# Selective scan with experts on 8 cores: one ring of seven buffers for dBu, h and h*C, delta in a ring of six quarters, 3 of 16 products h*C on GpSimd, silu in halves, u*D put into PSUM by ScalarE

## The chip, the cores and the metric

The kernel runs on all 8 cores of one Trainium2 chip, without exchange between them: core 2b+j does half j of sequence b. The time is that of the slowest core, in microseconds of the device; lower is better. Before the change it is 4211.43 us (median of 3 runs, 4205.42 to 4250.64).

## What is computed

One layer of a state-space block (16 states per channel, 2048 inner channels, model width 1024) and a mixture of experts (16 routed, 2 taken per token; 2 shared), on 4 sequences of 4096 tokens:

```python
x_and_res = x @ W_in                                # 1024 -> 2 x 2048
xi, res = jnp.split(x_and_res, 2, axis=-1)
xc = conv(xi, conv_w, 4 taps, causal, per channel) + conv_b
xi = silu(xc)                                       # called u below
Bm, Cm = jnp.split(xi @ W_xproj, 2, axis=-1)        # 16 + 16 columns
delta = softplus(xi @ W_dt + b_dt)
A = -exp(A_log)
def step(h, inp):
    dA = exp(d_i[:, None, :] * A[None, :, None])
    h = h * dA + d_i[:, None, :] * B_i[:, :, None] * u_i[:, None, :]
    y_i = sum(h * C_i[:, :, None], axis=1)
y = ys + xi * D_param
y = y * silu(res)
x = layernorm(x + y @ W_out)
# then: scores, softmax, top 2, x + routed + shared experts, layernorm
```

A core owns 2048 tokens. It walks 4096: a first half of 2048 that only builds up the state h (zeros, with a flag of 0, for the cores that own the start of a sequence), and a second half for which y is made.

## The kernel before, in words

Time is cut into 16 chunks k of 256 tokens (`TA`); chunks 0 to 7 (`PK`) are the first half, chunks 8 to 15 the second, "real" one. The 2048 channels are 16 tiles of 128; four tiles make a quarter of 128 x 1024 values (`QW`). A chunk has 64 steps: four quarters q of 16 states n. A step `st` handles one state of one quarter. `NR0` = 512 is the first real step.

What one step issues, engine by engine:

- GpSimd (`pool_front`, L522) multiplies du (= delta*u) of the quarter by the broadcast row B of state n into one of `NB` = 3 buffers `dBu`. It waits that the scan has freed the buffer. After n = 8 it prepares the next quarter (`prepare`: du by L442, and zt = delta*A of the first token, L445). After n = 13 it makes the next quarter's 16 carried-in states (`carry_in`, L459 to L467), for which it waits on an Exp by ScalarE (`first_decay`, L800). After the dBu of step 27 of a chunk it casts u of the next chunk to bf16 (`cast_u`, L433).
- ScalarE (`act_front`) does, in this order in each step: `keep_carry(st)` (L829, the last token's h is kept; in the second half it waits for the product), `decay(st+2)` (L817, exp(delta*A) into PSUM, three steps ahead in the first half), `give_carry(st+2)` (L838, the carried state into column 0 of dBu), then `dense(k, s)`: the evacuation of whatever group of matmuls stands in this step. After n = 11 comes `first_decay` of the next quarter. At step 26 it does the silu of the four quarters of u of chunk k+1, at steps 12 and 26 those of res.
- VectorE (`dve_front`) runs the scan (L942: h = decay*h + dBu) over 4 x 256 columns; in the second half it writes h over the decay in PSUM and then makes the product h*C in one of `NY` = 2 buffers `ym` (L952). At the first step of the next quarter it makes `combine`: u*D added in PSUM (L918, four instructions) and times silu(res) (L930).
- TensorE (`pe_front`) runs at each step first the group that `stage_at` names, then, in the second half, the accumulation of the product into the PSUM area `YB` by a product with the identity (L728, two of 512 columns). Its queue is in order, so the group of step s+1 stands behind the accumulation of step s.

The groups are those of the next chunk (k+1): input projection `xi` (L680, steps 0, 3, ..., 21), convolution `cv` (L692, steps 2, 5, ..., 23), `bc` = B and C (L701, step 30), `dt` = delta (L710, 16 groups at steps 32 to 59, about every 1.8th); and, in real chunks, `rs` = res of the same chunk (L680, steps 1, 4, ..., 22). Each goes to one of two PSUM banks and is evacuated by ScalarE in the same step of its own order. Chunk 0 has all of them 14 steps later, and part of its own `dt` groups in its steps (`LATE`). Weights are streamed by SyncE from bf16 copies in memory into rings of three (`x`) and two (`cv`, `dt`).

Semaphores alone bind the engines; the order on each is written out by hand in these functions. The lines that matter most:

```python
for key in stage_at(k, s):
    run(key)                                   # TensorE: the group of this step
if k >= 0 and is_real(k):
    te.wait_ge(s_ym, r + 1)                    # then the product of this step
```

```python
keep_carry(st)                                 # ScalarE, one step
decay(st + 2)
give_carry(st + 2)
dense(k, s)                                    # waits for the group of this step
if n == (12 if k == 0 else 11) and q + 1 < NQ:
    first_decay(q + 1)
```

## Time and profile before

| | |
|---|---|
| median of the runs | 4211.43 us |
| the profiled execution | 4194.85 us, span 4193.3 us (its slowest core, core 7; cores 4142.5 to 4193.3) |
| busy, share of the span | TensorE 2616.4 us (62%), VectorE 3296.4 (79%), ScalarE 2085.7 (50%), GpSimd 2779.4 (66%) |
| mean granted clock of TensorE | 0.846 on core 7, 0.845 on both dies |
| chain that ended last | VectorE 38%, issue 27%, GpSimd 11%, TensorE 10%, DMA 9%, ScalarE 2% |

The span has four stretches: a start of 124 us, the first half of the scan (512 steps, to about 1524 us), the second half (512 steps, to about 3556 us), and output projection, router and experts (637 us), which the change leaves alone but for how many token tiles are fetched early (`NPRE`). In the slices of the page VectorE is at eight to nine tenths in both halves; GpSimd is at nine tenths in the first half and six in the second. A busy share tells how much an engine worked, not which wait ended last.

### The profile page before, as it was taken

To read this page: it belongs to the slowest core of one execution; us is meant where nothing else is said; L and a number is where in the kernel's file an instruction comes from. 1 tells how busy PE (TensorE), PEld (TensorE's weight loads), DVE (VectorE), ACT (ScalarE), POOL (GpSimd) and SP (SyncE) were. 2 spreads that over 40 slices of the span, in tenths; PEclk is the share of its full clock that TensorE was granted. 3 is DMA by queue.
4 is the path that set the end of the run, shared out by engine and by line. 5 is a ranking of instruction groups with operands and counts; after the bars stand their busy time and mean duration, and the time that the engine had idled before them with its cause. 6 is when DMAs were issued, how large, how long until landed. Compare 5 with 4: busy or idle time off the path is not lost.

```text
span 4193.3 us, 57121 instructions; the slowest of 8 cores (4142.5 to 4193.3 us)
## 1 busy us (share of the span) xinstructions
PE 2616.4 (62%) x12773; PEld 1473.4 (35%) x12773; DVE 3296.4 (79%) x2266; ACT 2085.7 (50%) x4748; POOL 2779.4 (66%) x1556
## 2 busy tenths in 40 slices
PE   3354544444434467776777877777787665867870
PEld 2243332333323343343433434344443321433430
DVE  1678888888888898978989999898998999542227
ACT  2566666666666665445554645545455443210210
POOL 1889999999999986656666676666666665011012
PEclk8777776777767689989999999999999999888985
DMA  7653546635444356663736546464441321214976
GB/s 158 172 173 117 159 118 169 162 114 160 124 140 129 89 141 116 148 140 77 171 99 149 146 98 164 107 151 116 123 119 54 81 61 70 101 61 169 304 280 201
DMA packets 197735, 569.57 MB, mean 136 GB/s; under 512 B 21624, under 2 KB 87928, under 8 KB 175248
## 3 DMA queue, kind: packets, MB, share of 16 engines
q1 hardware_dynamic: 164736, 433.44, 33.7%
q0 software_dynamic: 32656, 132.36, 15.0%
q8 instruction: 117, 1.92, 0.2%
q14 instruction: 226, 1.85, 0.2%
HBM read 529.25 MB, written 154.14 MB: 163 GB/s over the span
## 4 chain that ended last, share of the span: by engine, by line
DVE 38%; issue 27%; POOL 11%; PE 10%; DMA 9%; ACT 2%; DVEq 1%; another core or an unknown queue 1%; POOLq 0%; SPq 0%; ACTq 0%
DVE PP L942 23%; DVE ym L942 8%; POOL dBu L522 8%; PE PP L1180 3%; DVE ym L952 2%; DMA RA<-wbx 2%; PE PP L1074 2%; DMA RA<-wbd 1%; PE PP L728 1%; DVE PP L918 1%; PE PP L1131 1%; DMA r<-xs 1%; DMA RA<-W_inx 1%; PE PP L710 1%
## 5 line engine op out<-in xcount | busy, mean ns | idle before, releaser
L522 POOL TENSOR_TENSOR dBu<-du,bcl 128x1020 f32<-128x1020 f32 x1024 | 2377.3, 2346 | 449.9 <-DVE PP L942 449.3
L942 DVE TENSOR_TENSOR_SCAN ym<-PP,dBu 128x1024 f32<-128x1024 f32 x512 | 1168.0, 2289 | 288.3 <-POOL dBu L522 263.3
L728 PE MATMUL PP<-ym,sid 128*128 128x512 f32 x2048 | 1048.8, 638 | 485.9 <-DVE ym L952 485.7
L942 DVE TENSOR_TENSOR_SCAN PP<-PP,dBu 128x1024 f32<-128x1024 f32 x512 | 1171.5, 2288 | 64.6 <-POOL dBu L522 52.4
L817 ACT ACTIVATE PP<-d,negA 128x1020 f32<-128x1020 f32 x1024 | 1124.8, 1099 | 2.3 <-issue 1.2
L710 PE MATMUL PP<-xib,RA 128*128 128x256 bf16 x4096 | 580.9, 305 | 310.6 <-ACT d L771 218.3
L952 DVE TENSOR_TENSOR ym<-PP,bcl 128x1024 f32<-128x1024 f32 x512 | 626.7, 1224 | 114.7 <-DVE PP L942 79.5
L728 PEld LDWEIGHTS PP<-ym,sid 128*128 128x128 f32 x2048 | 364.7, 198 | 966.6 <-issue 963.5
L710 PEld LDWEIGHTS PP<-xib,RA 128*128 128x128 bf16 x4096 | 438.1, 109 | 501.3 <-issue 414.4
L680 PE MATMUL PP<-xb,RA 128*128 128x256 bf16 x3072 | 450.7, 310 | 111.8 <-ACT d L771 35.8
L829 ACT ACTIVATE carry<-PP 128x4 f32<-128x4 f32 x512 | 88.4, 173 | 857.5 <-DVE ym L952 857.3
L680 PEld LDWEIGHTS PP<-xb,RA 128*128 128x128 bf16 x3072 | 339.6, 111 | 265.9 <-issue 190.2
L692 PE MATMUL PP<-xiraw,RA 128*128 128x256 bf16 x1024 | 168.6, 319 | 296.3 <-ACT xiraw L748 292.2
L829 ACT ACTIVATE carry<-ym 128x4 f32<-128x4 f32 x448 | 93.0, 208 | 422.0 <-DVE ym L942 420.8
L692 PEld LDWEIGHTS PP<-xiraw,RA 128*128 128x128 bf16 x1024 | 108.5, 111 | 378.2 <-issue 354.9
L838 ACT ACTIVATE dBu<-hc 128x4 f32<-128x4 f32 x1024 | 197.1, 193 | 0.0
L1242 ACT ACTIVATE r<-PP 128x1024 bf16<-128x1024 bf16 x48 | 49.0, 1024 | 278.6 <-PE PP L1166 278.6
L1180 PE MATMUL PP<-RA,r 128*128 128x512 bf16 x768 | 178.7, 387 | 9.2 <-DVE r L1446 8.1
L1446 DVE COPY r<-PP 128x1024 f32<-128x1024 f32 x48 | 58.7, 1225 | 158.4 <-DMA ys<-r 86.4
L984 POOL DMA_INDIRECT RA<-wre,widx x16 | 15.2, 948 | 228.9 <-PE PP L1180 228.1
L977 POOL DMA_INDIRECT xs<-r,posi x32 | 31.1, 973 | 189.6 <-DVE widx L1434 181.2
L442 POOL TENSOR_TENSOR du<-d,RA 128x1024 f32<-128x1024 f32 x64 | 150.5, 2351 | 1.6 <-ACT d L795 1.6
(149 smaller groups left out, 1821.5 us busy)
## 6 DMA issues: line engine op xcount, KB each, us to landing
RA<-wbd SPq DMA_DIRECT2D x120, 1024.0 KB, 6.5
RA<-wbx SPq DMA_DIRECT2D x184, 512.0 KB, 4.2
bcl<-bc_hbm SPq DMA_DIRECT2D x128, 256.0 KB, 6.8
wre<-Wre POOLq DMA_DIRECT2D x16, 2048.0 KB, 18.1
RA<-wbc SPq DMA_DIRECT2D x120, 256.0 KB, 3.0
ys<-r SPq DMA_DIRECT2D x48, 512.0 KB
xs<-g SPq DMA_DIRECT2D x26, 768.0 KB, 6.8
bcl<-bc_hbm SPq DMA_DIRECT2D x128, 128.0 KB, 5.2
```

What stands on the lines that cost most here:

```text
L442: ge.tensor_tensor(du[q % 2][:], quarter(d_b[k % 2], qd), quarter(u_b[k % 2], qd), ALU.mult).then_inc(s_du, 1)
L522: ge.tensor_tensor(ct3(dBu[st % NB][:])[:, :, 1:TA], ct3(du[q % 2][:])[:, :, 1:TA], bcl[n][:, 1:TA].rearrange("p (o t) -> p o t", o=1) .br ...
L680: mm = te.matmul(b[:, c * TA:(c + 1) * TA], wx[j % NX][:, (c * 8 + q) * 128:(c * 8 + q + 1) * 128], xb[k % 2][:, q * TA:(q + 1) * TA], sta ...
L692: mm = te.matmul(b[:, c * TA:(c + 1) * TA], wcv[j % NCV][:, (c * 4 + tap) * 128:(c * 4 + tap + 1) * 128], xr3[:, 2 * p + c, tap:tap + TA], ...
L710: mm = te.matmul(b[:, 0:TA], wdt[j % NDT][:, (c * CT + q) * 128:(c * CT + q + 1) * 128], xib[:, q * TA:(q + 1) * TA], start=(q == 0), stop ...
L728: mm = te.matmul(YB[:, zb * 512:(zb + 1) * 512], sid128[:], ym[r % NY][:, zb * 512:(zb + 1) * 512], start=(n == 0), stop=(n == NST - 1))
L817: se.activation(out=ct3(dec[b])[:, :, 1:TA], in_=ct3(quarter(d_b[k % 2], q % 4))[:, :, 1:TA], func=AF.Exp, scale=negA[:, n:n + 1]).then_in ...
L829: se.activation(out=carry[:, s * QC:(s + 1) * QC].rearrange("p (c o) -> p c o", o=1), in_=ct3(src)[:, :, TA - 1:TA], func=AF.Copy, scale=( ...
L838: se.activation(out=ct3(dBu[st % NB][:])[:, :, 0:1], in_=hc[q % 2][:, n * QC:(n + 1) * QC].rearrange("p (c o) -> p c o", o=1), func=AF.Cop ...
L942: ve.tensor_tensor_scan(out=hout, data0=dec[b], data1=dBu[st % NB][:], initial=0.0, op0=ALU.mult, op1=ALU.add).then_inc(s_scan, 1)
L952: ve.tensor_tensor(ct3(ym[r % NY][:]), ct3(dec[b]), bcl[n][:, TA:2 * TA].rearrange("p (o t) -> p o t", o=1) .broadcast_to([128, QC, TA]), ...
L1180: mm = te.matmul(pb[2 * (i % 2) + h], xT_r[i % 3][:, k * 128:(k + 1) * 128], wslot_e[b % 3][:, k * D + h * 512:k * D + (h + 1) * 512], sta ...
```

## The change

- One ring `hb` of `NB` = 7 buffers takes the place of `dBu` (3) and `ym` (2). dBu is made in a buffer, the scan reads it, the product h*C is made in the same buffer, TensorE accumulates from it. A buffer is free when TensorE has accumulated it (first half: when its last column is kept).
- The products of n = 1, 6 and 11 of each quarter (`POOL_N`) are made by GpSimd, which does so `LAG` = 4 steps later in its order: after the dBu of n = 5, 10 and 15. For these the scan writes h into the ring's buffer and not into PSUM. TensorE waits for each product in the order of the steps, whoever makes it.
- u*D: ScalarE writes it into `YB` at the first step of a quarter (`seed_y`, four instructions, after `give_carry`, ahead of `dense`), once the quarter before is combined. TensorE's accumulations of a quarter all add to it (a product once at the start sets the banks' state); the first waits for it. `combine` keeps only the multiplication by silu(res).
- delta is kept in a ring of six quarters (`dring`) in place of two whole chunks.
- For chunks 8 to 15: the silu of u is made in two halves, at steps 13 and 26; the cast to bf16 by GpSimd in two halves, ahead of the dBu of steps 22 and 36; `bc` at step 38, `dt` at steps 39, 40, 41, 43, 44, 46, 47, 49, 50, 51, 53, 54, 56, 57, 59, 60. The silu of the first half of res moves from step 12 to 13.
- For chunks 0 to 7 ScalarE makes the cast, after the four silus at step 26.
- At the start GpSimd issues two fetches of `dt` weights at its steps 0 and 1, no longer ahead of its first `prepare`; `NPRE` is 8, was 10.

```diff
@@ -35,13 +35,15 @@
...
-NPRE = 10
+NPRE = 8
...
-NB = 3
-NY = 2
+NB = 7
+LAG = 4
+ND = 6
+POOL_N = (1, 6, 11)
@@ -70,8 +72,15 @@
...
+def bc_step(k):
+
+    return 38 if k + 1 >= PK else 30 + shift(k)
+
+
 def dt_step(k, c):
+    if k + 1 >= PK:
+        return 39 + (23 * c) // 16
     return 46 + c if k == 0 else 32 + (29 * c) // 16
@@ -86,7 +95,7 @@
...
-        if f == 30:
+        if s == bc_step(k):
@@ -136,6 +145,21 @@
...
+
+
+def on_pool(r):
+
+    return r % NST in POOL_N
+
+
+def n_pool(r):
+
+    return r // NST * len(POOL_N) + sum(r % NST >= n for n in POOL_N)
+
+
+def n_dve(r):
+
+    return r + 1 - n_pool(r)
@@ -202,7 +226,7 @@
...
-    d_b = [sf(f"d{i}", [128, CT * TA], F32) for i in range(2)]
+    dring = sf("dring", [128, ND * QW], F32)
...
@@ -285,6 +307,7 @@
...
+    d_of = lambda q: dring[:, (q + 2) % ND * QW:((q + 2) % ND + 1) * QW]
...
@@ -401,6 +427,28 @@
...
+    def u_cast(e, k):
+
+        if is_real(k):
+            e.wait_ge(s_xibr, 4 * (k - PK + 1))
+        else:
+            e.wait_ge(s_xib, 4 * (k + 1))
+
+    def product_done(e, r):
+
+        if on_pool(r):
+            e.wait_ge(s_yp, n_pool(r))
+        else:
+            e.wait_ge(s_ym, n_dve(r))
+
+    def buffer_free(e, st):
+
+        p = st - NB
+        if p >= NR0:
+            e.wait_ge(s_ya, p - NR0 + 1)
+        elif p >= 0:
+            e.wait_ge(s_car, p + 1)
+
     def load_g(sy, j):
@@ -425,12 +473,19 @@
...
-        def cast_u(k):
-            if k >= 1:
-                ge.wait_ge(s_mm, USE[("dt", k - 1, CT - 1)] + 1)
-            for qd in range(4):
+        def cast_u(k, half):
+            ge.wait_ge(s_mm, USE[("dt", k - 1, CT - 1)] + 1)
+            for qd in (2 * half, 2 * half + 1):
                 ge.wait_ge(s_u, 4 * k + qd + 1)
-                ge.tensor_copy(quarter(xib, qd), quarter(u_b[k % 2], qd)).then_inc(s_xib, 1)
+                ge.tensor_copy(quarter(xib, qd), quarter(u_b[k % 2], qd)).then_inc(s_xibr, 1)
+
+        def product(st):
+            r, n = st - NR0, st % NST
+            ge.wait_ge(s_scan, st + 1)
+            ge.wait_ge(s_car, st + 1)
+            ge.tensor_tensor(ct3(hb[st % NB][:]), ct3(hb[st % NB][:]),
+                             bcl[n][:, TA:2 * TA].rearrange("p (o t) -> p o t", o=1)
+                             .broadcast_to([128, QC, TA]), ALU.mult).then_inc(s_yp, 1)
...
@@ -491,10 +546,7 @@
...
-        cast_u(0)
...
-        for p in range(2, 4):
-            cast_weights(("dt", 0, 2 * p))
@@ -502,26 +554,26 @@
...
             q, n = st // NST, st % NST
-            if k == 0 and s in (12, 28):
-                for p in range(2):
-                    cast_weights(("dt", 0, (8 if s == 12 else 12) + 2 * p))
+            if k == 0 and s in (0, 1, 12, 13, 28, 29):
+                cast_weights(("dt", 0, {0: 4, 1: 6, 12: 8, 13: 10, 28: 12, 29: 14}[s]))
             if k == 2 and s == 2:
...
                 ge.dma_start(out=wbx[8 + s // 8], in_=W_inx[8 + s // 8]).then_inc(s_wres, 16)
-            if s == 28 + shift(k) and k + 1 < NK:
-                cast_u(k + 1)
+            if PK <= k + 1 < NK and s in (22, 36):
+                cast_u(k + 1, s // 36)
             if s == 40 and k + 2 < NK:
...
             ge.wait_ge(s_du, q + 1)
-            if st >= NB:
-                ge.wait_ge(s_scan, st - NB + 1)
-            ge.tensor_tensor(ct3(dBu[st % NB][:])[:, :, 1:TA], ct3(du[q % 2][:])[:, :, 1:TA],
+            buffer_free(ge, st)
+            ge.tensor_tensor(ct3(hb[st % NB][:])[:, :, 1:TA], ct3(du[q % 2][:])[:, :, 1:TA],
                              bcl[n][:, 1:TA].rearrange("p (o t) -> p o t", o=1)
                              .broadcast_to([128, QC, TA - 1]), ALU.mult).then_inc(s_dbu, 1)
+            if st - LAG >= NR0 and on_pool(st - LAG - NR0):
+                product(st - LAG)
             if n == 5:
@@ -529,6 +581,9 @@
...
                     carry_in(q + 1)
+        for st in range(NS - LAG, NS):
+            if on_pool(st - NR0):
+                product(st)
@@ -558,7 +613,7 @@
...
-                    sy.wait_ge(s_ym, last - NR0 + 1)
+                    product_done(sy, last - NR0)
...
@@ -652,9 +708,9 @@
...
-                if s == 32 + shift(k):
+                if s == bc_step(k) + 2:
...
-                if s == 34 + shift(k):
+                if s == bc_step(k) + 4:
...
@@ -714,6 +770,11 @@
...
+        for zb in range(2):
+            for i in range(4):
+                mm = te.matmul(YB[:, zb * 512 + i * 128:zb * 512 + (i + 1) * 128], sid128[:], sid128[:],
+                               start=(i == 0), stop=(i == 3))
+        mm.then_inc(s_bits, 1)
@@ -721,13 +782,13 @@
...
                     n = s % NST
-                    te.wait_ge(s_ym, r + 1)
-                    if n == 0 and r >= NST:
-                        te.wait_ge(s_g, r // NST)
+                    product_done(te, r)
+                    if n == 0:
+                        te.wait_ge(s_yd, r // NST + 1)
                     for zb in range(2):
                         mm = te.matmul(YB[:, zb * 512:(zb + 1) * 512], sid128[:],
-                                       ym[r % NY][:, zb * 512:(zb + 1) * 512],
-                                       start=(n == 0), stop=(n == NST - 1))
+                                       hb[(k * NSTEP + s) % NB][:, zb * 512:(zb + 1) * 512],
+                                       start=False, stop=(n == NST - 1), skip_group_check=True)
                     mm.then_inc(s_ya, 1)
@@ -750,9 +811,9 @@
...
-                    se.wait_ge(s_xib, 4 * (k - 1))
+                    u_cast(se, k - 2)
...
-                        se.wait_ge(s_cb, 16 * (k - 2 - PK + 1))
+                        se.wait_ge(s_yd, 4 * (k - 2 - PK + 1))
@@ -765,10 +826,12 @@
...
-                if k >= 2:
-                    se.wait_ge(s_z, 4 * (k - 1))
-                    se.wait_ge(s_dA, (k - 1) * NSTEP)
-                se.activation(out=d_b[k % 2][:, p * TA:(p + 1) * TA], in_=b[:, 0:TA],
+                q = 4 * k + p // 4
+                if q >= ND:
+                    se.wait_ge(s_du, q - ND + 1)
+                    se.wait_ge(s_z, q - ND + 1)
+                    se.wait_ge(s_dA, (q - ND + 1) * NST)
+                se.activation(out=d_of(q)[:, p % 4 * TA:(p % 4 + 1) * TA], in_=b[:, 0:TA],
@@ -776,12 +839,19 @@
...
-        def silu_u(k):
-            se.wait_ge(s_ev, USE[("cv", k, 7)] + 1)
-            for qd in range(4):
+        def silu_u(k, half):
+            se.wait_ge(s_ev, USE[("cv", k, 4 * half + 3)] + 1)
+            for qd in (2 * half, 2 * half + 1):
                 se.activation(out=quarter(u_b[k % 2], qd), in_=quarter(u_b[k % 2], qd),
                               func=AF.Silu).then_inc(s_u, 1)
-            if k + 1 < NK:
+            if not is_real(k):
+                if k >= 1:
+                    se.wait_ge(s_mm, USE[("dt", k - 1, CT - 1)] + 1)
+                for qd in (2 * half, 2 * half + 1):
+                    se.wait_ge(s_u, 4 * k + qd + 1)
+                    se.activation(out=quarter(xib, qd), in_=quarter(u_b[k % 2], qd),
+                                  func=AF.Copy).then_inc(s_xib, 1)
+            if half == 1 and k + 1 < NK:
                 se.wait_ge(s_mm, USE[("cv", k, 7)] + 1)
...
@@ -805,8 +875,11 @@
...
-                se.wait_ge(s_ym, st - NR0 - 1)
-                se.wait_ge(s_car, st - 1)
+                if on_pool(st - 2 - NR0):
+                    se.wait_ge(s_scan, st - 1)
+                else:
+                    se.wait_ge(s_ym, n_dve(st - 2 - NR0))
+                    se.wait_ge(s_car, st - 1)
@@ -815,29 +888,42 @@
...
             se.activation(out=ct3(dec[b])[:, :, 1:TA],
-                          in_=ct3(quarter(d_b[k % 2], q % 4))[:, :, 1:TA],
+                          in_=ct3(d_of(q))[:, :, 1:TA],
                           func=AF.Exp, scale=negA[:, n:n + 1]).then_inc(s_dA, 1)
...
             se.wait_ge(s_scan, st + 1)
-            if st >= NR0:
-                se.wait_ge(s_ym, st - NR0 + 1)
+            in_psum = st >= NR0 and not on_pool(st - NR0)
+            if in_psum:
+                se.wait_ge(s_ym, n_dve(st - NR0))
             if st >= NSTEP:
                 se.wait_ge(s_hc, st // NST + 1)
-            src = dec[decay_slot(st)] if st >= NR0 else h_b[st % 2][:]
+            src = dec[decay_slot(st)] if in_psum else hb[st % NB][:]
             se.activation(out=carry[:, s * QC:(s + 1) * QC].rearrange("p (c o) -> p c o", o=1),
...
             q, n = st // NST, st % NST
-            if st >= NB:
-                se.wait_ge(s_scan, st - NB + 1)
+            buffer_free(se, st)
             se.wait_ge(s_hc, q + 1)
-            se.activation(out=ct3(dBu[st % NB][:])[:, :, 0:1],
+            se.activation(out=ct3(hb[st % NB][:])[:, :, 0:1],
                           in_=hc[q % 2][:, n * QC:(n + 1) * QC].rearrange("p (c o) -> p c o", o=1),
                           func=AF.Copy).then_inc(s_pad, 1)
+
+        def seed_y(q):
+            k, qd, r = q // 4, q % 4, q - 4 * PK
+            if r == 0:
+                se.wait_ge(s_scan, max(t for t in range(NR0) if decay_slot(t) == 2) + 1)
+            else:
+                se.wait_ge(s_g, r)
+            for c in range(QC):
+                ct = qd * QC + c
+                ins = se.activation(out=YB[:, c * TA:(c + 1) * TA],
+                                    in_=u_b[k % 2][:, ct * TA:(ct + 1) * TA],
+                                    func=AF.Copy, scale=Dp_c[:, ct:ct + 1])
+            ins.then_inc(s_yd, 1)
@@ -851,15 +937,14 @@
...
             if k + 1 < NK:
-                if s == 26 + shift(k):
-                    silu_u(k + 1)
+                for half in range(2):
+                    if s == (13 if half == 0 and k + 1 >= PK else 26) + shift(k):
+                        silu_u(k + 1, half)
             if k >= 0 and is_real(k):
-                if s == 12:
-                    silu_res(k, 0)
-                    silu_res(k, 1)
-                if s == 26:
-                    silu_res(k, 2)
-                    silu_res(k, 3)
+                for half in range(2):
+                    if s == (13, 26)[half]:
+                        silu_res(k, 2 * half)
+                        silu_res(k, 2 * half + 1)
@@ -879,12 +964,15 @@
...
                 give_carry(st + 2)
+            if st >= NR0 and n == 0:
+                seed_y(q)
             dense(k, s)
...
         ve.memset(xr3[:, :, 0:3], 0.0).then_inc(s_halo, 1)
+        ve.wait_ge(s_bits, 1)
         for i in range(3):
@@ -911,17 +999,8 @@
...
         def combine(q):
-            k, qd, r = q // 4, q % 4, q - 4 * PK
+            qd, r = q % 4, q - 4 * PK
             ve.wait_ge(s_ya, NST * (r + 1))
-            for c in range(QC):
-                ct = qd * QC + c
-                ve.scalar_tensor_tensor(
-                    out=YB[:, c * TA:(c + 1) * TA],
-                    in0=u_b[k % 2][:, ct * TA:(ct + 1) * TA],
-                    scalar=Dp_c[:, ct:ct + 1],
-                    in1=YB[:, c * TA:(c + 1) * TA],
-                    op0=ALU.mult, op1=ALU.add).then_inc(s_cb, 1)
-            ve.wait_ge(s_cb, QC * (r + 1))
             ve.wait_ge(s_sr, r + 1)
@@ -936,20 +1015,15 @@
...
             ve.wait_ge(s_pad, st + 1)
-            if st >= 2 and r < 0:
-                ve.wait_ge(s_car, st - 1)
-            hout = dec[b] if r >= 0 else h_b[st % 2][:]
-            ve.tensor_tensor_scan(out=hout, data0=dec[b], data1=dBu[st % NB][:], initial=0.0,
+            by_dve = r >= 0 and not on_pool(r)
+            hout = dec[b] if by_dve else hb[st % NB][:]
+            ve.tensor_tensor_scan(out=hout, data0=dec[b], data1=hb[st % NB][:], initial=0.0,
                                   op0=ALU.mult, op1=ALU.add).then_inc(s_scan, 1)
...
                 combine(q - 1)
-            if r >= 0:
+            if by_dve:
                 ve.wait_ge(s_scan, st + 1)
-                if r < 2:
-                    ve.wait_ge(s_car, NR0 - 1 + r)
-                if r >= NY:
-                    ve.wait_ge(s_ya, r - NY + 1)
-                ve.tensor_tensor(ct3(ym[r % NY][:]), ct3(dec[b]),
+                ve.tensor_tensor(ct3(hb[st % NB][:]), ct3(dec[b]),
                                  bcl[n][:, TA:2 * TA].rearrange("p (o t) -> p o t", o=1)
...
```

## Rows read from the trace of the kernel before

**Rows 1.** Busy time by stretch: start, first half, second half, rest (us, instructions, clock, DMA)

```profile
124.00:1524.00 1400.00, 651.56 (x3888) 457.43 (x3888) 1166.58 (x512) 910.84 (x1995) 1335.70 (x727) 0.72 0.48 139
1524.00:3556.00 2032.00, 1507.66 (x6300) 789.90 (x6300) 1844.80 (x1180) 1047.97 (x2555) 1344.52 (x721) 0.94 0.46 116
```

**Rows 2.** Waits of the second half (total us, times, longest us)

```profile
POOL dBu L522 <- DVE PP L942: 449.3, 304, 7.6
...
POOL zt L459 <- ACT zt L800: 121.8, 22, 9.2
...
DVE PP L942 <- POOL dBu L522: 52.4, 9, 7.5
```

**Rows 3.** Timeline of VectorE over a quarter's change (start us, us, instruction)

```profile
2429.88 2.29 DVE L942 TENSOR_TENSOR_SCAN PP<-PP,dBu 128x1024 f32<-128x1024 f32 x1
...
2434.08 1.23 DVE L930 TENSOR_TENSOR g<-PP,sres 128x1024 bf16<-128x1024 f32 x1 [0.24 <-DVE PP L918]
...
2436.35 2.29 DVE L942 TENSOR_TENSOR_SCAN PP<-PP,dBu 128x1024 f32<-128x1024 f32 x1
...
2439.95 2.29 DVE L942 TENSOR_TENSOR_SCAN PP<-PP,dBu 128x1024 f32<-128x1024 f32 x1
```

**Rows 4.** Timeline of VectorE in the first half: six scans that wait for nothing

```profile
788.89 13.80 DVE L942 TENSOR_TENSOR_SCAN ym<-PP,dBu 128x1024 f32<-128x1024 f32 x6 [1.10 <-POOL dBu L522]
```

**Rows 5.** Timeline of GpSimd in a quarter of the second half, around carry_in

```profile
2455.50 2.35 POOL L442 TENSOR_TENSOR du<-d,RA 128x1024 f32<-128x1024 f32 x1
...
2471.20 2.35 POOL L522 TENSOR_TENSOR dBu<-du,bcl 128x1020 f32<-128x1020 f32 x1 [1.25 <-DVE PP L942]
...
2478.34 0.32 POOL L459 TENSOR_TENSOR zt<-zt,carry 128x64 f32<-128x64 f32 x1 [4.79 <-ACT zt L800]
...
2479.43 9.27 POOL L522 TENSOR_TENSOR dBu<-du,bcl 128x1020 f32<-128x1020 f32 x4
```

**Rows 6.** Timeline of ScalarE at n = 11 and 12 of that quarter

```profile
2476.20 0.17 ACT L829 ACTIVATE carry<-PP 128x4 f32<-128x4 f32 x1 [1.64 <-DVE ym L952]
...
2477.71 0.24 ACT L800 ACTIVATE zt<-zt 128x64 f32<-128x64 f32 x1
...
2481.32 0.45 ACT L771 ACTIVATE d<-PP,colt 128x256 f32<-128x256 f32 x1
```

**Rows 7.** Timeline of TensorE in the second half, back to back and after idle times

```profile
2381.91 1.04 PE L692 MATMUL PP<-xiraw,RA 128*128 128x256 bf16 x8
...
2469.00 1.96 PE L728 MATMUL PP<-ym,sid 128*128 128x512 f32 x4
2470.79 1.91 PE L710 MATMUL PP<-xib,RA 128*128 128x256 bf16 x16
...
2419.30 6.37 PE L728 MATMUL PP<-ym,sid 128*128 128x512 f32 x8 [8.92 <-DVE ym L952]
...
2532.08 3.57 PE L710 MATMUL PP<-xib,RA 128*128 128x256 bf16 x16 [4.23 <-DMA RA<-wbd]
```

**Rows 8.** Timeline of ScalarE at step 26 of a real chunk

```profile
2406.45 1.28 ACT L782 ACT_TABLE_LOAD   x1
...
2407.74 3.90 ACT L782 ACTIVATE RA<-RA 128x1024 f32<-128x1024 f32 x4
...
2414.00 1.28 ACT L817 ACT_TABLE_LOAD   x1
```

**Rows 9.** Timeline of GpSimd in a chunk of the first half, around the cast

```profile
734.10 3.98 POOL L433 CAST xib<-RA 128x1024 bf16<-128x1024 f32 x4 [3.82 <-ACT RA L782]
...
742.66 0.31 POOL L459 TENSOR_TENSOR zt<-zt,carry 128x64 f32<-128x64 f32 x1
```

**Rows 10.** Timeline of ScalarE there: the Exp that carry_in waits for

```profile
739.50 0.24 ACT L800 ACTIVATE zt<-zt 128x64 f32<-128x64 f32 x1
```

**Rows 11.** Timeline of GpSimd at the start

```profile
116.63 0.53 POOL L426 DMA_DIRECT2D RA<-W_dtx  x1 [22.16 <-DMA wbd<-RA]
...
121.70 27.63 POOL L522 TENSOR_TENSOR dBu<-du,bcl 128x1020 f32<-128x1020 f32 x12 [0.21 <-issue]
```

21 lines of the change are left out of this document (12 added, 9 removed).

## The prediction

> **What bounds the kernel now.** I read the stretches first, then the waits, then the timelines. The first half's 512 steps take 1400 us with GpSimd busy for 1335.7 of them; the second half's take 2032 us with VectorE busy for 1844.8 and GpSimd for 1344.5 [rows 1]. So each half has its own bound, and the change shifts work from the engine that bounds the second one. The waits of the second half agree: GpSimd waits 449.3 us for scans to free its three buffers, but also 121.8 us for the Exp ahead of carry_in; VectorE waits for dBu only nine times, 52.4 us in all [rows 2]. The timelines give pitches, which count more than durations since neighbours overlap. From scan to scan it is 3.60 us, with a quarter's change in between 6.47, so combine costs 2.87 [rows 3]. A scan that waits for nothing takes 13.80/6 = 2.30 us [rows 4]. A chunk's work on VectorE is thus 64 x 3.60 + 4 x 2.87 = 241.9 us, of 2032/8 = 254 measured; 12 us are stalls, the longest (7.5 us, [rows 2]) after the silus of step 26.
>
> **VectorE's work after.** Per quarter: 12 steps of 3.60; n = 0 with a scan (2.30), one multiplication by silu(res) (about 1.2, [rows 3]) and a product (1.2), 4.7 together; three bare scans, 6.9. Sum 54.8 us, 219 a chunk, 23 less than now. Over eight chunks 183 us would be gained if nothing made VectorE wait. What follows asks whether that holds.
>
> **The steps around n = 11.** Let T be the end of scan 11, whose product GpSimd now makes. In this order:
> - ScalarE keeps the carry, makes decay and pad of step 13, and the Exp of the next quarter; from the carry's start that took until 2477.95, 1.75 us [rows 6], and with the group's evacuation (0.45, [rows 6]) and the handover about 2.7. So the Exp ends at T+2.7, if TensorE isn't late.
> - GpSimd has had dBu 13 for long and waits (now 4.79 us there, [rows 5]). Its next dBu starts 2479.43 - 2477.95 = 1.5 us after the Exp. It then makes dBu 14 and 15 (9.27/4 = 2.32 each) and only then product 11, priced as the same kind of instruction, 2.35 [rows 5]. That ends 8.5 us after the Exp: T+11.2. However deep the ring is, carry_in takes GpSimd's lead away here in every quarter.
> - TensorE stands at product 11 all that time, in order. Behind it are the group of step 12 and the products of 12 to 15, which VectorE has ready. Each accumulation or group of 16 takes about 1.8 us back to back, a convolution's group of 8 about 1.1 [rows 7].
> - ScalarE stands in `dense(12)` for that group: accumulation 1.8, group 1.9, handover and evacuation 0.7, then carry, decay and pad of step 15, 1.6 (2477.71 - 2476.20 and a handover, [rows 6]). VectorE wants them at T+10.8 (three steps of 3.60) and gets them at T+17.4. A stall of 6.6 us. Where step n = 12 has a group, that is steps 12, 44 and 60, three quarters of four.
> - combine must have product 15 accumulated. Unstalled it would start at T + 4 x 3.60 + 2.30 = T+16.7; five accumulations and the groups between them end at T+20.2 or later.
>
> **A chunk quarter by quarter** (from combine to combine; without stalls T comes at 54.8 - 16.7 = 38.1 us). *Steps 48 to 63*: scan 15 at T+17.5, scan 16 ends at T+23.4, TensorE is done by then. T is 38.6, since `seed_y` delays the first accumulation and the carries of n = 1 to 4 a little: 62.1 us. *Steps 32 to 47*: groups at n = 6 to 9, 11, 12, 14, 15. With 3.6 us of TensorE in most of these steps it is late by T, the evacuation of step 11 too, so the Exp is at T+4.6, product 11 at T+13.0, and the accumulation of 15 at T+27.6: 37.9 + 27.7 = 65.6. *Steps 16 to 31*: none at n = 12, but at step 26 ScalarE still has two silus of u and two of res between two table loads. Now there are four and two (1.28, 3.90, ..., 1.28 in [rows 8]). Without two of them the Exp is at T+7.7, product 11 at T+16.1, five accumulations end at T+25.3: 64.5. *Steps 0 to 15*: a group in every step, the Exp at T+4.9, product 11 at T+13.3; the evacuation of step 13 comes after three more of TensorE's pieces and then four silus (5.2 us with a table load) and a load back, so decay 16 is ready only at T+29.5: 39.0 + 32.1 = 71.1. Sum 263.3 against 254 now. In chunk 15 there are only the groups of res and no silu of u; the same walk gives 64 + 61 + 58 + 58 = 241 against 253.
>
> Second half at full clock: 7 x 9.3 - 12 = +53.
>
> **The clock.** In the second half TensorE's clock is granted at 0.94 of full speed [rows 1]. After a wait of 8.92 us two accumulations took 6.37 us, where two back to back take 3.7; after one of 4.23 us a group took 3.57, where others take 1.91 [rows 7]: the lower level, 1.2 GHz. The change puts a wait of 6 to 9 us into each of 32 quarters, right before the chain that counts. The price is from 0 (clock kept, as in the accumulation of 1.96 us, [rows 7]) to 2.6 us each; I take 1.66, the nearer row's 3.57 - 1.91: +53. By the Trainium skill, "TensorE: Matmul & The Clock Gate", Part 1, the array falls to half clock when it idles and comes back after a while of work; the rows agree. Its remark that the ramp costs under 1% of a typical kernel's span would cap this term at 42 us, the sum at 4296.
>
> **The first half.** The cast leaves GpSimd (3.98 us and a wait of 3.82 before it, [rows 9]), which looks like 7.8 us a chunk. But GpSimd then arrives sooner at carry_in, which waits for the Exp; and ScalarE has four casts more (3.9 us, as its silus, [rows 8]) between silu and that Exp. It ends at 739.74 now [rows 10], then at 743.65, and carry_in starts at 744.1 and not 742.66 [rows 9]: +1.4 us a chunk, six times; +1.9 in chunk 0; about -0.5 in chunk 7, whose next chunk is cast the other way. The ring of seven helps no more than one of three where GpSimd is the bound. At the start GpSimd no longer stands at the fetch issued at 116.63 [rows 11] before `prepare`, but it stands there one dBu later, and the casts by ScalarE cost about 2.7 us: second dBu at 120 rather than 124, -4. Together +6.
>
> The seed's start matmuls lie in the wait for the first weights; four seed instructions and a smaller combine are in the walk; two token tiles fetched later (`NPRE`) have the output projection of the tiles before them as cover, 0. SyncE's fetch of bcl waits for GpSimd's product, with weight fetches queued behind it; those are due steps later, 0. `dt` groups 1.44 steps apart leave less room for their weights: 0 to +5 us a chunk, taken as 0. GpSimd's sixteen dBu, three products, prepare and carry_in are some 49 us of 54.8: not the bound by sum.
>
> **Sum**: 4194.85 + 53 + 53 + 6 = 4307 us. The profiled execution is 0.4% under the median of 4211.43 shown; I leave that in the range.
>
> **Rivals.** *(a) The other side: the ring covers it.* GpSimd keeps a lead over n = 11 to 15, so that product 11 comes within some 4 us of its scan, and the group of step 12 in time for scan 15 (that is the point: 6.6 us earlier than walked). Then only today's stalls stay: 4194.85 - 183 + 6 = 4018. For it: GpSimd's 449.3 us of waiting for buffers [rows 2] go, and 49 us fit into 54.8. Against it: the buffers don't free ScalarE from `dense(12)`. The Trainium skill, "Perfetto Trace Analysis", Optimizing Scalar/DVE Operations, says that moving work from a saturated VectorE even to GpSimd may make sense, and warns of the port that they share. *(b) Half of it.* ScalarE's two steps of slack and the removed combine cancel the lateness: stalls of 6 us a quarter and no clock loss give 243 a chunk, 4194.85 - 84 + 6 = 4117; with 8.6, as walked but without the clock, 4254. *(c) Slower than the forecast.* Late accumulations also meet the weights' fetches and the low clock twice a quarter (the wait of the first accumulation for `seed_y` is some 5 us too): +1.7 in 24 quarters and +5 in 7 chunks: 4383. It decides wherever TensorE's queue and not VectorE ends last. *(d)* The change does less than it says: product on GpSimd slower than dBu (in place, VectorE writing the same memory). At 3.5 us instead of 2.35 it adds 1.2 in 32 quarters: 4344.
>
> **Chances.** Forecast, with (d), 0.48; (c) 0.14; (a) 0.17; (b) 0.21, of which 0.14 near 4250 and below, within 1% of the median (4169 to 4253, about what a measurement here can tell from no change), and 0.07 faster. So faster 0.24, same 0.14, slower 0.62. The range leaves out the ideal case and the far end of (c): 4110 to 4385; the forecast's own is 4254 (no loss of clock) to 4350.
>
> **What would show it.** GpSimd's product for n = 11 starts right after a dBu, about 9 us after the scan; TensorE idle for 6 to 9 us before the accumulation of n = 11, then half clock; ScalarE's wait for TensorE in `dense` high, which is small now; a stall of VectorE ahead of scan 15 and 16; no gap there in chunk 15's last quarters. GpSimd's wait for VectorE small. A chunk at 263 to 275 us. Wrong if VectorE's gaps at n = 15 are under 2 us, a chunk is under 245 us, or the first half's chunks fall below 173.

## The result and the profile after

The changed kernel takes 4419.56 us (median of four runs, 4411.96 to 4421.41) beside 4208.43 for the one before on the same chip: 1.0493 times as long, 95% interval 1.0447 to 1.054. The forecast was 4307 with 4385 as its upper end; direction and mechanism came out, the size didn't: +211 us, not +96 (profiled execution against profiled execution, as the forecast was summed: 4421.41 - 4194.85 = +227 for +112). In some executions the cores of one die are granted a lower clock and take longer: ratios, the times of runs 2, 3 and 8 and the ranges over cores leave these out, the other medians have them in. This is the head of its page (busy time; then busy tenths in 40 slices):

```profile
span 4419.8 us, 56272 instructions; the slowest of 8 cores (4351.3 to 4419.8 us)
...
PE 2653.0 (60%) x12745; PEld 1523.3 (34%) x12789; DVE 3133.7 (71%) x2042; ACT 2157.6 (49%) x4910; POOL 2962.5 (67%) x1620
...
DVE  1878887878888857677686777767787788652227
...
PEclk7777676776776888888888888889888887888985
...
PE 29%; issue 21%; POOL 16%; DVE 15%; DMA 10%; ACT 7%; another core or an unknown queue 1%; POOLq 1%; DVEq 0%; ACTq 0%; SPq 0%
```

VectorE lost 163 us of work against before (3296.4) and the span still grew by 226.5: an engine that has less to do and takes longer is waiting. Its digits show where, after the middle (6 and 7 where before had 8 and 9), and PEclk has mostly an 8 there where before had a 9. The last line is the chain that ended last: TensorE leads it with 29%, where before it was VectorE with 38%. The stretches (start to first scan, first half, second half, rest) answer to [rows 1]:

```profile
0.00:106.00 106.00, 46.63 (x288) 33.69 (x288) 14.88 (x74) 30.27 (x49) 14.58 (x24) 0.81 0.75 167
106.00:1515.00 1409.00, 644.39 (x3920) 456.27 (x3920) 1167.57 (x512) 939.41 (x2026) 1309.12 (x699) 0.72 0.49 141
1515.00:3787.00 2272.00, 1554.58 (x6304) 839.96 (x6304) 1685.80 (x961) 1087.72 (x2683) 1556.85 (x817) 0.84 0.41 103
```

The second half took 2272 us against 2037 (1525 to 3562; [rows 1] leaves off its last 6): +235. It starts 10 us earlier than before. Waits of the second half (total, times, longest), which answer to [rows 2]:

```profile
DVE PP L1020 <- ACT hb L911: 447.1, 101, 27.4
PE PP L789 <- POOL hb L486: 393.0, 46, 16.4
ACT dring L834 <- PE PP L766: 384.7, 112, 12.7
POOL zt L514 <- ACT carry L903: 289.2, 22, 34.0
...
PE PP L789 <- ACT PP L923: 186.4, 32, 13.6
POOL hb L572 <- PE PP L789: 72.0, 56, 24.9
...
PE PP L736 <- DMA RA<-wbx: 57.0, 7, 26.5
```

Read as a ring: VectorE waits for ScalarE's `give_carry` (L911), which ScalarE issues right after the decay (447), ScalarE for TensorE's group (385), TensorE for GpSimd's product (393). GpSimd's old wait for VectorE's scans (449.3 in [rows 2]) is gone, as the ring of seven promises; nobody needed it. One quarter, steps 32 to 47 of a chunk, from combine to combine. GpSimd and TensorE:

```profile
2583.75 0.33 POOL L500 TENSOR_TENSOR zt<-dring,negA 128x64 f32<-128x64 f32 x1
2584.04 4.64 POOL L572 TENSOR_TENSOR hb<-du,bcl 128x1020 f32<-128x1020 f32 x2
2588.64 2.33 POOL L486 TENSOR_TENSOR hb<-hb,bcl 128x1024 f32<-128x1024 f32 x1
...
2609.89 0.32 POOL L514 TENSOR_TENSOR zt<-zt,carry 128x64 f32<-128x64 f32 x1 [12.02 <-ACT carry L903]
...
2610.98 4.63 POOL L572 TENSOR_TENSOR hb<-du,bcl 128x1020 f32<-128x1020 f32 x2
2615.57 2.35 POOL L486 TENSOR_TENSOR hb<-hb,bcl 128x1024 f32<-128x1024 f32 x1
```

```profile
2591.12 3.47 PE L789 MATMUL PP<-hb,sid 128*128 128x512 f32 x4 [3.73 <-POOL hb L486]
...
2618.06 3.75 PE L789 MATMUL PP<-hb,sid 128*128 128x512 f32 x4 [9.43 <-POOL hb L486]
2621.60 2.17 PE L766 MATMUL PP<-xib,RA 128*128 128x256 bf16 x16
```

ScalarE and VectorE in the same quarter (T, the end of scan 11, is 2602.67 + 2.28 = 2604.95):

```profile
2609.26 0.25 ACT L870 ACTIVATE zt<-zt 128x64 f32<-128x64 f32 x1
...
2624.04 0.47 ACT L834 ACTIVATE dring<-PP,colt 128x256 f32<-128x256 f32 x1 [11.93 <-PE PP L766]
```

```profile
2564.76 1.23 DVE L1009 TENSOR_TENSOR g<-PP,sres 128x1024 bf16<-128x1024 f32 x1 [5.75 <-PE PP L789]
...
2599.12 2.30 DVE L1020 TENSOR_TENSOR_SCAN PP<-PP,hb 128x1024 f32<-128x1024 f32 x1 [2.91 <-ACT hb L911]
...
2602.67 2.28 DVE L1020 TENSOR_TENSOR_SCAN hb<-PP,hb 128x1024 f32<-128x1024 f32 x1
...
2626.11 2.30 DVE L1020 TENSOR_TENSOR_SCAN PP<-PP,hb 128x1024 f32<-128x1024 f32 x1 [8.92 <-ACT hb L911]
...
2634.39 1.23 DVE L1009 TENSOR_TENSOR g<-PP,sres 128x1024 bf16<-128x1024 f32 x1 [2.45 <-PE PP L789]
```

The Exp ends at T+4.6 and the product of n = 11 (behind carry_in and two dBu) at 2617.92, T+13.0: to a tenth what the walk of this quarter had. Then comes the accumulation at 1.2 GHz (3.75 us, 1.88 at 2.4 GHz), the group ScalarE stands for, scan 15, and combine at T+29.4 (walked 27.7 + 1.66). What the walk did not have is the line at 2591.12: the product of n = 6 is late too, behind `prepare` and two dBu, and costs TensorE 3.73 us of waiting, the lower level once more, and VectorE the 2.91 us at 2599.12. T came at 40.2 us after combine, not 37.9.

Distances from combine to combine, read off VectorE's timeline, in us (L930 before, L1009 after; the starred quarters have a copy of the later stages' weights, issued by GpSimd at n = 5, that shows):

| chunk | before | after |
|---|---|---|
| k = 8 | –, 67.7, 65.0*, 60.5 | –, 95.1*, 67.8, 65.7 |
| k = 9 | 79.2*, 67.8, 60.5, 60.5 | 97.9*, 67.0, 69.6, 75.8* |
| k = 12 | 61.9, 68.1, 60.5, 60.5 | 74.1, 68.3, 70.8, 73.4* |
| k = 14, no copies | 61.9, 67.9, 60.5, 60.5 = 250.8 | 74.3, 66.8, 66.3, 65.7 = 273.1 |
| k = 15, no next chunk | 61.4, 61.9, 60.5, 60.5 = 244.3 | 67.3, 62.8, 58.4, 53.6 = 242.1 |

Chunk 15 has no dt groups, and there the saving of VectorE's work is all there in the last quarter: 53.6, with a pitch of 3.53 us from scan to scan (3.60 before).

### The profile page after: what moved, and what is told of

Its sections match the earlier page's. It is cut to its first block, busy times and chain, and to the rows that moved or that the text cites. A ratio compares the mean times of both kernels' runs of the same rounds, so it can differ in the third digit from the quotient of the medians.

```text
span 4419.8 us, 56272 instructions; the slowest of 8 cores (4351.3 to 4419.8 us)
## 1 busy us (share of the span) xinstructions
PE 2653.0 (60%) x12745; PEld 1523.3 (34%) x12789; DVE 3133.7 (71%) x2042; ACT 2157.6 (49%) x4910; POOL 2962.5 (67%) x1620
## 4 chain that ended last, share of the span: by engine, by line
PE 29%; issue 21%; POOL 16%; DVE 15%; DMA 10%; ACT 7%; another core or an unknown queue 1%; POOLq 1%; DVEq 0%; ACTq 0%; SPq 0%
PE PP L789 13%; POOL hb L572 11%; DVE hb L1020 7%; PE PP L766 5%; DVE PP L1020 4%; PE PP L736 4%; DMA RA<-wbx 3%; PE PP L1255 3%; POOL hb L486 2%; DMA r<-xs 2%; DMA RA<-wbd 2%; POOL du L497 2%; DVE hb L1026 1%; PE PP L1149 1%; PE PP L1206 1%
## 5 line engine op out<-in xcount | busy, mean ns | idle before, releaser
L572 POOL TENSOR_TENSOR hb<-du,bcl 128x1020 f32<-128x1020 f32 x1024 | 2370.8, 2347 | 73.3 <-PE PP L789 72.0
L1020 DVE TENSOR_TENSOR_SCAN hb<-PP,hb 128x1024 f32<-128x1024 f32 x608 | 1387.2, 2287 | 281.0 <-POOL hb L572 188.9
L789 PE MATMUL PP<-hb,sid 128*128 128x512 f32 x2048 | 1084.7, 668 | 623.5 <-POOL hb L486 393.0
L1020 DVE TENSOR_TENSOR_SCAN PP<-PP,hb 128x1024 f32<-128x1024 f32 x416 | 952.4, 2289 | 471.3 <-ACT hb L911 447.1
L890 ACT ACTIVATE PP<-dring,negA 128x1020 f32<-128x1020 f32 x1024 | 1124.9, 1099 | 1.2 <-issue 0.8
L789 PEld LDWEIGHTS PP<-hb,sid 128*128 128x128 f32 x2048 | 402.7, 213 | 1071.5 <-issue 1068.2
L1026 DVE TENSOR_TENSOR hb<-PP,bcl 128x1024 f32<-128x1024 f32 x416 | 509.3, 1224 | 40.1
L486 POOL TENSOR_TENSOR hb<-hb,bcl 128x1024 f32<-128x1024 f32 x96 | 225.4, 2348 | 251.0 <-ACT carry L903 250.9
L514 POOL TENSOR_TENSOR zt<-zt,carry 128x64 f32<-128x64 f32 x64 | 20.3, 318 | 446.4 <-ACT carry L903 353.3
L911 ACT ACTIVATE hb<-hc 128x4 f32<-128x4 f32 x1024 | 197.4, 193 | 0.0
L497 POOL TENSOR_TENSOR du<-dring,RA 128x1024 f32<-128x1024 f32 x64 | 151.1, 2361 | 48.7 <-ACT dring L865 48.7
```

Of the source, the lines that this page charges most:

```text
L486: ge.tensor_tensor(ct3(hb[st % NB][:]), ct3(hb[st % NB][:]), bcl[n][:, TA:2 * TA].rearrange("p (o t) -> p o t", o=1) .broadcast_to([128, Q ...
L497: ge.tensor_tensor(du[q % 2][:], d_of(q), quarter(u_b[k % 2], qd), ALU.mult).then_inc(s_du, 1)
L572: ge.tensor_tensor(ct3(hb[st % NB][:])[:, :, 1:TA], ct3(du[q % 2][:])[:, :, 1:TA], bcl[n][:, 1:TA].rearrange("p (o t) -> p o t", o=1) .bro ...
L789: mm = te.matmul(YB[:, zb * 512:(zb + 1) * 512], sid128[:], hb[(k * NSTEP + s) % NB][:, zb * 512:(zb + 1) * 512], start=False, stop=(n == ...
L890: se.activation(out=ct3(dec[b])[:, :, 1:TA], in_=ct3(d_of(q))[:, :, 1:TA], func=AF.Exp, scale=negA[:, n:n + 1]).then_inc(s_dA, 1)
L911: se.activation(out=ct3(hb[st % NB][:])[:, :, 0:1], in_=hc[q % 2][:, n * QC:(n + 1) * QC].rearrange("p (c o) -> p c o", o=1), func=AF.Copy ...
```

## The experiments

Each edit is against the changed kernel unless it says otherwise. "Before" is the kernel before on the same chip in the same hour.

**1. No products on GpSimd.**

```
-POOL_N = (1, 6, 11)
+POOL_N = ()
...
```

> The changed kernel with POOL_N empty: VectorE makes all 16 products h*C; ring, delta ring, schedule, seed by ScalarE as changed. Theory A (product 11 stands behind carry_in on GpSimd, which waits for ScalarE's Exp; TensorE stands at it, ScalarE in dense, VectorE for ScalarE): the boundary stalls of 6 to 16 us a quarter go, VectorE has 58.5 us of work a quarter, 32 x 58.5 = 1872 plus some 150 us of other stalls for the second half: about 4170 us. Theory B (what costs is late weights: dt groups closer together and 2 MB copies in their way): no effect on that, 4380 or more. Theory C (GpSimd has too much work): also near 4170, so A and C are told apart by the next two.

Measured: 4129.98 us beside 4213.17, ratio 0.9827 (0.977 to 0.9885). The quarters of chunk 14 are 61.6, 61.3, 57.7, 58.5 = 239.1. So the ring, the silu in halves and the seed together are a gain of 1.7% (1.2 to 2.3), and the three products a loss of some 280 us (1.0493 - 0.9827 of 4210).

**2. Products at n = 1, 5, 9.**

```
-POOL_N = (1, 6, 11)
+POOL_N = (1, 5, 9)
```

> The changed kernel with POOL_N = (1, 5, 9): the same three products a quarter on GpSimd, but the last one after dBu 13, ahead of carry_in, none behind it. Theory A: TensorE no longer stands at a product that waits for the Exp: second half shorter by 6 us or more in each of 32 quarters, 4150 to 4230 us. Theory B and C: the same work on every engine, so 4400 to 4430.

Measured: 4191.08 us (4175.17 to 4230.49) beside 4213.17, ratio 0.9951 (0.989 to 1.0012). As much work on GpSimd as in the change, and some 230 us less (1.0493 - 0.9951 of 4210). All of it is in the second half: the first combine comes when it did, and from there to the last it is 1939 to 1957 us (cores 0 to 3) where the change has 2168 to 2196.

**3. Only the Exp for carry_in earlier.**

```
-            if n == (12 if k == 0 else 11) and q + 1 < NQ:
+            if n == (12 if k == 0 else 9) and q + 1 < NQ:
                 first_decay(q + 1)
```

> The changed kernel with the Exp of the next quarter (first_decay) after n = 9 in place of n = 11, products at 1, 6, 11 as changed. Theory A: GpSimd goes through carry_in without waiting, has dBu 15 before scan 11 ends, and product 11 ends about 3 us after scan 11 and not 11 to 13: 4150 to 4230 us; in the first half the wait before carry_in may shrink too (up to 8 us a chunk). Theory B and C: 4390 or more.

Measured: 4166.22 us, one run, beside 4213.17, so 0.989 of it and without an interval. TensorE's wait for GpSimd's products halves:

```profile
PE PP L789 <- POOL hb L486: 197.1, 50, 7.7
```

The same three products at the same three places, some 250 us less. About 180 of them are in the second half (1985 to 2016 us from first to last combine, over the eight cores): what cost there was that n = 11 stood behind a carry_in that waited for ScalarE. The other 70 are in the first half, which has no products at all: the first combine comes at 1509 to 1525 us and not at 1585 to 1602. GpSimd is the bound there, and its wait for ScalarE's `keep_carry` ahead of carry_in (L514) falls from 64.1 us to 10.5. The expectation named this ("up to 8 us a chunk"); every later run with the Exp after n = 9 has it.

**4. The copies in the first half.** `tail_weights` copies W_out (4 MB), the shared experts' weights (4 MB) and the 16 routed experts' (2 MB each) in quarters 33 and on; here they start in quarter 8.

```
-                tail_weights(q - 4 * PK - 1)
+                tail_weights(q - 8)
```

> The changed kernel with the copies of the later stages' weights (W_out, shared experts, 16 x 2 MB of routed experts) issued from quarter 8 on, in the first half, and not in the second. Theory B: dt and x weights come in time in the second half, so the steps 48 to 63 fall from 73 to 66 us and the outliers of 95 and 98 us go: 4419 - 130 = 4290 or less. Theory A alone: 4380 to 4420; with both, about 4300 with stalls of VectorE at n = 15 left as they are. In the first half GpSimd is the bound and issues 22 copies of 0.54 us more there: +12 us.

Measured: 4437.07 (4452.48 and 4421.65) beside 4213.17, ratio 1.0558 (1.047 to 1.0647). From the first combine to the last it took 2097 to 2100 us (cores 0 to 3), some 84 less than the change's average, and the long quarters went. But the first combine came at 1659 to 1695, some 85 us later: the copies cost about as much in the first half as in the second, and the time stays. Run 9 has the same second half without them.

**5. Both cures: n = 1, 5, 9 and the Exp after n = 9.** (Edits 2 and 3.)

> The changed kernel with both cures of the last two runs that cured: products at n = 1, 5, 9 on GpSimd and the Exp after n = 9. Theory A says that each alone takes away the same wait (product 11 behind carry_in), so together they give little more: 4130 to 4170. If instead each took away a cost of its own (4420 - 204, 4420 - 223), the two together would give about 3990.

Measured: 4079.32 beside 4194.26, ratio 0.9732 (0.9685 to 0.9779), under the expected 4130 to 4170. The two cures don't add in the second half, as expected (1911 to 1948 us from first to last combine, 1939 to 1957 in run 2); what puts the time under the range is the first half's 70 us of run 3. The second half is no shorter than in run 1, which has no products on GpSimd (1891 to 1928). The waits of TensorE for products and of ScalarE for groups, 393.0 and 390.0 over the whole span of the change:

```profile
ACT dring L834 <- PE PP L766: 179.2, 92, 13.0
...
PE PP L789 <- POOL hb L486: 106.7, 46, 6.8
```

**6. The same with the dt groups earlier and wider apart, 7. the same without products, 8. the change with earlier dt groups alone.** The common edit:

```
-    return 38 if k + 1 >= PK else 30 + shift(k)
+    return 30 + shift(k)
...
-    if k + 1 >= PK:
-        return 39 + (23 * c) // 16
     return 46 + c if k == 0 else 32 + (29 * c) // 16
...
```

The second half of the cast moves with them, from the dBu of step 36 to that of step 28.

> The same with the schedule of the kernel before for real chunks: bc at step 30, dt over steps 32 to 59, the second half of the cast ahead of dBu 28. Theory B as a second cost (dt groups every 1.44 steps leave their weights and TensorE too little room): steps 48 to 63 fall from about 68 to 60 us, 4060 to 4110 in all. If the spacing doesn't matter: as the run before, within 15 us.

> The same with no product on GpSimd (VectorE has 58 us of work a quarter, not 54). If VectorE's work is what is left: slower than the run before by up to 32 x 3.5 = 110 us, about 4090 + 50; if the products on GpSimd cost in TensorE's order what they save on VectorE, it is the faster of the two: 4060 to 4090.

> The changed kernel, products at 1, 6, 11 and Exp after n = 11 as changed, with bc at step 30 and dt over 32 to 59 alone. Theory B as the second cost: steps 48 to 63 fall from 73 to 60 to 64 us (no group at step 60 any more, weights in time), the rest stays: 4330 to 4370. If the spacing doesn't matter: 4400 to 4420.

Measured beside 4194.26: with the cures 4101.22, ratio 0.9777 (0.9735 to 0.9819), no difference from 5 that the intervals show; without products 4079.21, ratio 0.9732 (0.969 to 0.9774); the change with it alone 4400.23, one run, 1.0498 of the two of before (4188.95 and 4194.26), where the change has 1.0493.

So the whole time shows nothing of the spacing, but the second half of run 8 does. From first to last combine it takes 2113 to 2158 us on the eight cores, every core under the change's 2168 to 2196. Chunk 14, which has no copies, is as long as before (272.9 for 273.1); chunks 9 to 12, which have them, take 303.4, 274.6, 278.6 and 274.2 where the change has 310.3, 287.4, 290.2 and 286.6. The close spacing costs nothing by itself and 7 to 13 us a chunk where copies run. The two kernels ran on different chips; on the profiled cores the first combine came 9 us later in run 8 and what follows the last one took 644 us for 634, which hides half of the 40 us gained between.

And products on GpSimd (6) give nothing over none (7), with all else equal: 0.9777 and 0.9732.

**9. and 10. The copies after the recurrence,** in the change and in the kernel before. All copies but W_out's are issued behind the last scan. The whole time grows, as they lie bare; what counts is the second half.

```
-            if n == 5:
-                tail_weights(q - 4 * PK - 1)
+            if n == 5 and q == 4 * (NK - 1) + 1:
+                tail_weights(0)
...
```

> The changed kernel with the weight copies for the later stages taken out of the second half: W_out's in chunk 15, the shared and the 16 routed experts' after the scan, where they are in plain view (some 250 us more at the end), so only the second half is compared. Theory: what the walk missed is that these copies make TensorE's weights late, and that no slack hides it any more. The second half falls from 2272 us to 2272 - 116 = 2156, every chunk near 273 us. Rival (the walk is off at every quarter, copies or not): 2240 or more.

> The kernel before with the same removal. If the copies cost it as much as the changed kernel: second half 2037 - 116 = 1920. By its trace (chunk 14, without copies, 251 us; sum of the others above that 36): 2037 - 36 = 2001.

Measured, one run of each: 4700.65 and 4524.48. The second half of either:

```profile
1526.00:3702.00 2176.00, 1544.07 (x6304) 835.63 (x6304) 1682.81 (x961) 1088.69 (x2682) 1545.78 (x798) 0.85 0.30 87
```

```profile
1529.00:3532.00 2003.00, 1500.18 (x6304) 784.44 (x6304) 1846.82 (x1185) 1045.25 (x2554) 1333.27 (x701) 0.96 0.34 95
```

So the copies cost the second half 2272 - 2176 = 96 us in the change and 2037 - 2003 = 34 before, on the profiled cores. Over the eight cores, first to last combine, it is 84 on average in the change (2168 to 2196 against 2097 to 2100) and 34 before (1961 to 1990 against 1939 to 1942). Without them the change's second half is 173 us longer than that of before, chunks k = 9 to 13 at 275.6 to 277.3 against 251. How that shows in a line: while a copy of 2 MB is in flight, the `dt` weights that SyncE fetches take 18.3 us to land, where the median of the second half is 5.9, and TensorE stands. DMA issues of 2634 to 2670 (KB each, median us to landing), then from the same view of the whole second half, and TensorE:

```profile
wre<-Wre POOLq DMA_DIRECT2D x1, 2048.0 KB, 19.1
RA<-wbd SPq DMA_DIRECT2D x2, 1024.0 KB, 18.3
```

```profile
RA<-wbd SPq DMA_DIRECT2D x54, 1024.0 KB, 5.9
...
wob<-W_outx POOLq DMA_DIRECT2D x1, 4096.0 KB, 41.2
```

```profile
1643.19 3.22 PE L736 MATMUL PP<-xb,RA 128*128 128x256 bf16 x16 [26.47 <-DMA RA<-wbx]
...
2663.68 3.27 PE L766 MATMUL PP<-xib,RA 128*128 128x256 bf16 x16 [6.54 <-DMA RA<-wbd]
...
2693.96 3.57 PE L789 MATMUL PP<-hb,sid 128*128 128x512 f32 x4 [9.42 <-POOL hb L486]
```

The first of these lines is in the quarter of 95.1 us of chunk 8: W_out's copy was issued at 1599.76.

**11. Seed by VectorE.** Kernel 5, with u*D added in combine by VectorE as before and no `seed_y` on ScalarE.

```
+            for c in range(QC):
+                ct = qd * QC + c
+                ve.scalar_tensor_tensor(
+                    out=YB[:, c * TA:(c + 1) * TA],
+                    in0=u_b[k % 2][:, ct * TA:(ct + 1) * TA],
+                    scalar=Dp_c[:, ct:ct + 1],
+                    in1=YB[:, c * TA:(c + 1) * TA],
+                    op0=ALU.mult, op1=ALU.add).then_inc(s_cb, 1)
...
```

> Products at 1, 5, 9 and the Exp after n = 9 (4079 us), with u*D added by VectorE in combine as in the kernel before, nothing written to YB by ScalarE. VectorE has 1.7 us more a quarter: +54 us if it is what counts, 4130. The wait of 6 us of TensorE for the seed and the low clock after it go: -1.7 to -3 us a quarter, 4020 if that is what counts. I expect both and a result within 30 us of 4079.

Measured: 4127.34 beside 4227.95, ratio 0.9792 (0.973 to 0.9855), against 0.9732 for 5 on another chip, and 18 us over the expected range: the seed in PSUM is worth about 0.6%, within the width of the two intervals. That TensorE's wait for it (186.4 us of waits in the change) costs more than it gives is not what this run says.

**12. Kernel 5 without copies in a chunk's last quarter.**

```
-            if n == 5:
-                tail_weights(q - 4 * PK - 1)
+            if n == 5 and q % 4 < 3:
+                tail_weights(3 * (k - PK) + q % 4 - 1)
```

> The same kernel of 4079 us with the copies issued in the first three quarters of a chunk alone, none at the steps 48 to 63, where the dt weights are fetched. In that kernel these steps take 65 us with a copy and 57 without, the others hardly differ: 4 x 8 us less, 4040 to 4055. If a copy costs the same wherever it stands: 4075 to 4085.

Measured: 4053.33 beside 4227.95, ratio 0.9607 (0.9545 to 0.9669), as expected. The last quarters fell from 65 to 57; two long ones stayed, 92.4 and 76.0.

**13. Kernel 12 with the routed experts' copies first,** W_out's and the shared experts' in chunk 15.

```
+        def real_copy(q):
+            k, qd = q // 4, q % 4
+            if k == NK - 1:
+                return (1, 0, 3, 5)[qd]
+            j = 3 * (k - PK) + qd
+            return 6 + j if k >= PK and qd < 3 and j < NEXP else None
...
```

> The kernel with GpSimd's products at positions 1, 5 and 9, the decay's Exp after position 9, and the copies kept out of each chunk's last quarter (4053 us beside 4228 before), with the order of the copies changed: the routed experts' weights, 2 MB each, go first, in chunks 8 to 13, and W_out and the shared experts' weights in chunk 15. In the earlier order the second and third quarter of chunks 8 and 9 had one quarter of 92.4 us and one of 76.0 where the others have about 61: the theory is that the copies of W_out and of the shared experts' weights there meet SyncE's loads of wbx and wbd, and that the last quarter of the recurrence is untouched by them. Then those two come down to 61 and the time is about 4010 us if the tail does not wait for what is copied late, or 4053 and more if the wait reappears in chunk 15 or ahead of the experts. The rival, that the two quarters are long for a reason of their own at the start of the second half (loads of that stretch), leaves them at 90 and 75 and the time at 4053.

Measured: 4031.73 beside 4200.92, ratio 0.9571 (0.9499 to 0.9642), the fastest kernel of the study. TensorE's wait for `wbx` in the second half, in 12 and then here:

```profile
PE PP L736 <- DMA RA<-wbx: 39.0, 2, 28.2
```

```profile
PE PP L743 <- DMA RA<-wbx: 3.2, 2, 3.1
```

The two long quarters are 62.9 and 61.5. The last combine is at 3388.89 instead of 3422.82, although chunk 15's last quarter with its copy takes 60.5 instead of 53.7; of these 34 us what follows gives 9 back, 637.6 instead of 628.9.

**14. The change with TensorE kept busy before the product of n = 11,** by matmuls with a tile of zeros, `zer`, that leave the accumulator as it is.

```
+                    if n == 11:
+                        for _ in range(130):
+                            te.matmul(YB[0:64, 0:128], zer[:], ones[:], start=False, stop=False,
+                                      skip_group_check=True)
...
```

> The changed kernel with one addition: in every quarter, before TensorE waits for the product of position 11, it accumulates a tile of zeros by 130 matmuls of 128 columns into the first 64 rows of the open accumulator YB, which changes no value. They take some 7 us at full clock, of the 9.4 us for which TensorE stood before that product. If the lower clock that follows this idle stretch (3.57 us for the next accumulation instead of 1.9) is part of the loss, as my theory of what remains beyond the copies has it, each quarter gives back about 1.7 us, 32 times: about 54 us, so some 4365 us against 4420, and the accumulation of position 11 falls to about 1.9 us in the records. If the clock's share hides behind VectorE's next scan (rival: TensorE catches up by position 15), the single accumulation falls too but the time stays within 10 us of 4420. If the filling delays the product's own accumulation because it is still running when the product comes, the quarter grows and the time is above 4420.

Measured: 4410.14 beside 4200.92, ratio 1.0455 (1.0379 to 1.0532): no difference that these intervals show. From first to last combine it is 2130 to 2184 us, 25 less on average than in the change; chunk 14 is 273.1 to 273.7 on six cores, about as there, and 270.3 on two. TensorE around the filling:

```profile
2683.76 7.45 PE L791 MATMUL PP<-ones,zer 128*64 128x128 bf16 x130
2693.29 2.65 PE L797 MATMUL PP<-hb,sid 128*128 128x512 f32 x4 [2.09 <-POOL hb L487]
2695.74 2.93 PE L767 MATMUL PP<-xib,RA 128*128 128x256 bf16 x16
2698.51 5.32 PE L797 MATMUL PP<-hb,sid 128*128 128x512 f32 x12
```

The filling filled 7.45 us, and the lower level came all the same, later: 2693.29 to 2698.51 is 5.2 us, and in the change the same two pieces (2693.96 to 2699.11, the line above and its neighbour) took 5.15. So the run doesn't do what it was made for and leaves the clock's share open.

**15. and 16. Which of the three products costs.** First n = 11 alone on GpSimd, then n = 1 and 6 alone.

```
-POOL_N = (1, 6, 11)
+POOL_N = (11,)
```

> The changed kernel, of whose three products on GpSimd only that of position 11 is left; VectorE makes 1 and 6. My theory: this one product carries the loss. Each quarter pays 2 x 1.2 us more on VectorE and gets back what the product of position 6 cost (a wait of 3.73 us and an accumulation at the lower clock on TensorE, a stall of 2.91 us on VectorE in the quarter read). So the quarters stay within 1 us of 74, 67, 69.6 and 66, and the time lies between 4390 and 4430 beside 4420 for the changed kernel. The rival, that each of the three products costs alike, gives two thirds of what none of them gives (4130): about 4227.

```
-POOL_N = (1, 6, 11)
+POOL_N = (1, 6)
```

> The changed kernel with the products of positions 1 and 6 on GpSimd and that of position 11 by VectorE. My theory: no product stands behind carry_in, so the wait of 9.4 us is gone and a quarter is that of the kernel without GpSimd's products (61.3) less two products of VectorE (2.3), 59 us; what the product of position 6 makes late before the end of scan 11 is in reserve, up to 2.9 us a quarter. Time: 4130 - 32 x 2.3 = 4056 at best, 4130 if the product of position 6 costs as much as it saves. The rival (each product costs alike, some 97 us of 290) gives 4323.

Measured: 4399.41 beside 4216.33, ratio 1.0413 (1.0357 to 1.0469), and 4166.32, ratio 0.9894 (0.9856 to 0.9931). The one product of n = 11 has nearly the whole loss: its ratio is 0.8 points under that of all three and 5.9 over that of none. Chunk 14 with n = 11 alone is 276.8 (quarters of 73.4, 69.2, 67.4 and 66.8, the second 2 us off the expected 67), with 1 and 6 it is 239.0, with none 239.1. So what products 1 and 6 save, the lateness of 6 takes back (TensorE waits 5.46 us for it at 2468.45 in run 16, and the next accumulation took 3.75), and where copies run they cost besides: chunks 9 to 12 take 275.3, 252.4, 253.5 and 254.2 in run 16 and 266.7, 245.6, 245.8 and 243.6 in run 1. 16 is 36 us over its expected upper end, and its ratio 0.7 points over that of run 1.

**Where the time lies.** From the traces, read off VectorE's combines: when the first one comes, and how long it is from there to the last (us, lowest to highest over the eight cores; runs 2 and 4 over cores 0 to 3).

| kernel | first combine | first to last |
|---|---|---|
| before | 1574 to 1593 | 1961 to 1990 |
| change | 1585 to 1602 | 2168 to 2196 |
| 15, only n = 11 | 1585 to 1599 | 2140 to 2164 |
| 8, change with earlier dt groups | 1585 to 1600 | 2113 to 2158 |
| 9, change, copies last | 1584 to 1604 | 2097 to 2100 |
| 4, copies in the first half | 1659 to 1695 | 2097 to 2100 |
| 10, before, copies last | 1581 to 1594 | 1939 to 1942 |
| 3, Exp after n = 9 | 1509 to 1525 | 1985 to 2016 |
| 2, n = 1, 5, 9 | 1578 to 1586 | 1939 to 1957 |
| 16, n = 1 and 6 | 1573 to 1589 | 1924 to 1950 |
| 1, no products | 1573 to 1590 | 1891 to 1928 |
| 5, both cures | 1507 to 1519 | 1911 to 1948 |
| 7, as 6 without products | 1509 to 1525 | 1899 to 1930 |
| 13 | 1507 to 1530 | 1850 to 1870 |

## Why the forecast was right in kind and short in size

- **Product 11 stands behind carry_in.** Right, and it is the cause: run 3 leaves the product where it is and only lets carry_in start sooner, run 2 leaves carry_in and moves the product; they take some 180 and some 230 us out of the second half. Run 15 shows it alone, run 16 without it. In the quarter read the times after T were met to 0.1 us at the Exp and the product, and combine came at 29.4 for 29.36.
- **Rival (a), the ring covers it,** fell: TensorE's wait is 9.4 us a quarter, not 4. GpSimd's wait for buffers did go, without any effect. Runs 5 (4079) and 13 (4032) come near its 4018, but by another way, and that is luck: its 183 us were to come from VectorE's shorter work in the second half. Run 5's second half is only some 50 us shorter than that of before, and no shorter than run 1's with no product on GpSimd; 70 us come from the early Exp in the first half, and in run 13 the rest from the copies.
- **The term that was mis-sized: the copies.** The step said "`dt` groups 1.44 steps apart leave less room for their weights: 0 to +5 us a chunk, taken as 0". Without copies in flight the spacing costs nothing (chunk 14 of run 8); with them it costs 7 to 13 us a chunk, and the copies as a whole, which the term leaves out, more: GpSimd's copies delay SyncE's fetches. Run 9 measures 96 us in the second half (84 on average over the cores). The error was twofold. The walk's 263.3 us has no copies in it, and it was set against "254 now", which has: without copies a chunk of before is 250.8, 34 us over the half. And in the change TensorE leads the chain that ends last (29%, the page), so less of a late weight is absorbed; the same transfers cost 96. That this is why they cost more is argued; only the two costs are measured.
- **The walk itself:** chunk 14, without copies, took 273.1 where 263.3 + 4 x 1.66 = 269.9 was expected, the others 276. By quarters 74.3, 66.8, 66.3, 65.7 for 72.8, 66.2, 67.3, 63.8. The step that the walk lacks is the product of n = 6, late behind `prepare` and two dBu; the trace shows it, and runs 1 and 16 agree (two products fewer on VectorE, no gain). That this is the whole of what the walk lacks is not shown. 173 us between runs 9 and 10, where the walk, rid of its wrong base, gives 7 x (269.9 - 250.8) + (241 + 6.6 - 244.3) = 137: 36 short. Together 96 + 36 = 132, and the second half was 2272 - (2037 + 106) = 129 over the forecast.
- **A slip in rival (b).** It says "with 8.6, as walked"; the walk's 263.3 less 219 of work is 44 us a chunk, 11 a quarter. Its 4254 is the walk's 53 + 6 and stands; 8.6 a quarter would have given about today's 254 a chunk. Nothing else in the forecast uses it.
- **The clock.** The trace agrees with the row that the forecast took: 3.57 and 3.75 us for an accumulation after 9.4 us of idle time where 1.9 is usual, and the granted clock of the second half went from 0.94 to 0.84. It falls up to three times a quarter (first accumulation, n = 6, n = 11) and not once, as rival (c) had it in part. What the level costs in the end was not separated from the waits that bring it: run 14 failed to hold it, though its mean in the second half was 0.89, filling included. The forecast's +53 is neither shown nor refuted. That the ramp stays under 1% of a span, the remark of the Trainium skill that the forecast weighed ("TensorE: Matmul & The Clock Gate", Part 1), no run here could measure by itself.
- **Start and first half.** Forecast +6, measured -10: the second scan comes at 114.44 instead of 126.6 (-12, forecast -4), the chunks are 2.6 us longer in all, forecast +10. In sum: +113 = +129 - 16 over 4307.

**Open:** how the 36 us split between product 6 and the lower clock; a run with the Exp early and n = 6 moved only would tell. And what the early Exp alone gives the kernel before: that its first half has the same 70 us to give was not run. The runs were made on different chips, and those of 3, 8, 9 and 10 rest on one run each; the smaller differences named from them, 34 us for the copies before and 7 to 13 a chunk in run 8, are no surer than that.

## What to carry to other kernels

Before work is given to an engine with spare time, look at what stands ahead of it in that engine's own queue, and at who stands behind it in the consumer's: GpSimd had the time for three products, but one of them sat behind a wait for another engine, and TensorE, in order, held up the groups that the recurrence itself needs. Moving that wait (here: the Exp two steps earlier) or the product took the loss away; but no placing of the products tried here was faster than leaving them on VectorE (runs 6 and 7, and 2 and 16 beside 1), so the work was not worth moving. Read a gain by stretches before naming its cause: 70 us of every run with the early Exp lie in the first half, where no product was moved. And a walk that is set against a measured stretch must contain what the stretch contains; bulk transfers in the background are priced anew as soon as another queue becomes the one that ends last.

## What the runs showed of the hardware

- Copies from HBM to HBM on GpSimd's queue delay the fetches on SyncE's: with one of 2 MB in flight two weight fetches of 1 MB landed 18.3 us after issue (median of the second half 5.9), and with W_out's of 4 MB (41.2 us) TensorE stood 26.5 us for a fetch in the change and 28.2 us in run 12.
- Filling 7.45 of 9.5 us of TensorE's idle time with 130 small matmuls (128 columns into 64 rows) did not keep the level of 2.4 GHz over the remaining 2.09 us of waiting: the two pieces behind it took as long as with no filling.
- A product of two 128x1024 fp32 tiles takes GpSimd 2.35 us, and VectorE, which has one of them in PSUM, 1.23: with both cures the three moved products a quarter brought nothing that could be measured (runs 6 and 7: 0.9777 and 0.9732).
